# One transformer layer with routed experts on one core: row scatters at eight places instead of one, and a new order of the first keys and queries

## The reference

```
q,k,v = x @ qkv_w.T            16 heads of 16 channels
q,k   = rotary(q), rotary(k)   x*cos + rotate_half(x)*sin
attn  = softmax(q k^T / 4 + 8 * slope_h * min(0, key - query))
x1    = layernorm(x + (attn v) @ proj_w.T + proj_b)
shared= silu(x1 @ sW1 + sb1) @ sW2 + sb2
act   = sqrt(softplus(x1 @ routing_W.T + expert_bias));  top 2 of 8 experts
out   = layernorm(x1 + shared + sum over the 2 of act_e * expert_e(x1))
```

## Time and profile before

| | |
|---|---|
| median of the runs | 1753.69 us |
| the profiled execution's own time | 1758.38 us |
| its span | 1756.6 us |
| granted clock of PE, mean | 0.916 of full |
| PE busy | 1494.1 us, 85% |
| DVE busy | 1161.4 us, 66% |
| ACT busy | 1031.6 us, 59% |
| POOL busy | 723.8 us, 41% |
| first score product | 38.26 us |

### The profile page before, as it was taken

One profiled execution on the slowest core, in us unless ns is written; L12 is line 12 of the kernel. 1 busy time (PEld: TensorE's weight loads), 2 busy tenths in 40 slices (PEclk: granted clock), 3 DMA queues, 4 the chain that ended last, 5 costly groups with the idle time before them and its releaser, 6 DMA issues.

```text
span 1756.6 us, 33407 instructions
## 1 busy us (share of the span) xinstructions
PE 1494.1 (85%) x11096; PEld 812.6 (46%) x11096; DVE 1161.4 (66%) x2641; ACT 1031.6 (59%) x1766; POOL 723.8 (41%) x662
## 2 busy tenths in 40 slices
PE   3887989898898999999889998888999897977764
PEld 1433434444454454544445554444444454545643
DVE  5775767676877575666776776758767665533356
ACT  0265656565566576766656675656656675753633
POOL 0233354544435434343545535363354533232444
PEclk7699999899899999999999999999998998977887
DMA  5335243333343444444454545445454555436853
GB/s 181 100 118 160 81 123 101 105 115 111 96 135 122 138 137 148 134 143 140 134 167 155 163 138 165 149 144 164 141 152 148 177 163 178 122 117 190 272 187 118
DMA packets 189924, 251.74 MB, mean 143 GB/s; under 512 B 67837, under 2 KB 104794, under 8 KB 189754
## 3 DMA queue, kind: packets, MB, share of 16 engines
q1 hardware_dynamic: 177514, 216.96, 40.4%
q0 software_dynamic: 11520, 31.47, 5.6%
q10 hardware_dynamic: 720, 1.16, 0.2%
HBM read 157.78 MB, written 95.90 MB: 144 GB/s over the span
## 4 chain that ended last, share of the span: by engine, by line
PE 54%; DVE 14%; SPq 11%; DMA 8%; issue 7%; another core or an unknown queue 3%; ACT 2%; POOL 1%; ACTq 0%; DVEq 0%; POOLq 0%
PE pS L605 15%; PE pV L648 10%; DVE negm L893 6%; PE pG L670 5%; PE pG L781 3%; PE pG L679 3%; PE pS L611 3%; DMA rb<-d_rec 2%; DMA d_rec<-scr 2%; PE pG L773 2%; PE pG L692 2%; SPq L410 2%; PE pG L754 2%; SPq L454 2%
## 5 line engine op out<-in xcount | busy, mean ns | idle before, releaser
L893 DVE TENSOR_REDUCE negm<-pS 128x1 f32<-128x512 f32 x1024 | 660.2, 683 | 351.7 <-PE pS L611 296.8
L1294 ACT ACTIVATE ee<-pT,slp 128x512 f32<-128x512 f32 x1024 | 651.0, 684 | 271.3 <-PE pT L632 212.9
L605 PE MATMUL pS<-ka,qa 62*128 62x512 f32 x1024 | 491.8, 512 | 162.1 <-DVE negm L893 103.9
L626 PE MATMUL pT<-qa,ka 64*128 64x512 f32 x1024 | 489.9, 511 | 12.4 <-ACT ee L1294 11.4
L605 PEld LDWEIGHTS pS<-ka,qa 62*128 62x128 f32 x1024 | 199.9, 195 | 409.8 <-issue 361.9
L648 PE MATMUL pV<-ee,vv 128*32 128x512 f32 (+1 forms) x2048 | 295.9, 652 | 1.5 <-issue 1.2
L611 PE MATMUL pS<-mAB,tri 64*128 64x64 bf16 x2048 | 244.7, 201 | 0.0
L632 PE MATMUL pT<-mAB,tri 64*128 64x64 bf16 x2048 | 241.8, 199 | 0.0
L1450 POOL TENSOR_TENSOR raw<-raw,rope 128x512 f32<-128x512 f32 x60 | 76.8, 1280 | 366.5 <-DVE sh L923 366.5
L626 PEld LDWEIGHTS pT<-qa,ka 64*128 64x128 f32 x1024 | 198.0, 193 | 25.7 <-issue 13.2
L611 PEld LDWEIGHTS pS<-mAB,tri 64*128 64x128 bf16 x2048 | 120.5, 100 | 137.5 <-issue 99.2
(11 more groups left out here) (175 smaller groups left out, 2128.1 us busy)
## 6 DMA issues: line engine op xcount, KB each, us to landing
d_part<-parts SPq DMA_DIRECT2D x64, 512.0 KB
qa<-d_part SPq DMA_DIRECT2D x384, 64.0 KB
wb<-in_wb SPq DMA_DIRECT2D x88, 256.5 KB
xg<-d_x SPq DMA_DIRECT2D x88, 256.0 KB
d_y<-yb SPq DMA_DIRECT2D x88, 256.0 KB
ka<-d_part SPq DMA_DIRECT2D x128, 128.0 KB
xT<-in_xT SPq DMA_DIRECT2D x16, 512.0 KB
ka<-d_part SPq DMA_DIRECT2D x128, 64.0 KB
```

The source lines that it names most:

```text
L605: e.matmul(pS[:, k, :], qa[g % 4][r, i, t * 128:t * 128 + 128].bitcast(F32R), ka[g % 4][r, i, :].bitcast(F32R), start=True, stop=False)
L626: e.matmul(pT[:, k, :], ka[g % 4][r, i, kt * 128:kt * 128 + 128].bitcast(F32R), qa[g % 4][r, i, :].bitcast(F32R), start=True, stop=False)
L893: e.tensor_reduce(negm[:, g % 2, j, t + k:t + k + 1], pS[:, k, :], AX, ALU.max, negate=True).then_inc(s_max, 1)
L1294: e.activation(ee[:, w % 2, k, j, :], pT[:, k, :], ACT.Exp, scale=slp[:, 6, h:h + 1]).then_inc(s_exp, 1)
```

## The change

1. **Scatters.** `SCATTER` is now (78, ..., 85): one indirect DMA in each of eight slots. The waits before the first stay before the first.
2. **The start.** The key and query weights come in slices; the loads of `xT` and the first rows of `bpos` come earlier; masks are made on POOL behind the first two rotations. DVE does the rotations of i = 0, 1 and 2 of block 0, i = 1 directly behind i = 0 in tiles of its own (`raw_q`, `sh_q`, `parts_q`, which lie in `gg` and `bs`); i = 3 goes to POOL. `bpos` is made for four heads first (DVE), for the rest by ACT. Part of the row loads of groups 0 and 1 is issued by ACT.
3. **Idle products.** `warm(n)` makes n products of zeros (128 x 256) in front of the first real product, between products and around the wait before the first score.
4. **Later weights.** `LATE` is 11, the five preparations of `PREP` are at 18, 20 and 22, SP's part of them at 24. `load_xT(1)` is in slot 3.

```diff
-SCATTER = (81, 81)
+SCATTER = (78, 79, 80, 81, 82, 83, 84, 85)
-LATE, PREP, PADS = 3, 8, 40
+LATE, PREP, PADS = 11, (18, 20, 22, 24), 40
+WARM = (5, 6, 4, 4, 5)
...
+    def query_rows(e, g, some):
+        q_ = d_part[g // 4 % 2][0, 4 * (g % 4):4 * (g % 4) + 4]
+        for a in some:
+            for c in range(2):
+                r0 = 64 * c
+                e.dma_start(qa[g % 4][r0:r0 + 32, a, :], q_[2 * a + c, :, 0:1, :].broadcast_to([D, 2, T])
+                            ).then_inc(qk_in[g % 4], 16)
+            r0 = 64 * a + 32
+            e.dma_start(qa[g % 4][r0:r0 + 16, :, :], q_[a::2, :, 1, :].rearrange("a d t -> d a t")).then_inc(qk_in[g % 4], 16)
...
@@ stream of SP @@
+        def key_rows(g):
+            k_ = d_part[g // 4 % 2][1, 4 * (g % 4):4 * (g % 4) + 4]
+            for c in range(2):
+                r0 = 64 * c
+                e.dma_start(ka[g % 4][r0:r0 + 32, :, :], k_[c::2].rearrange("a d p t -> (d p) a t")).then_inc(qk_in[g % 4], 16)
+                e.dma_start(ka[g % 4][r0 + 32:r0 + 48, :, :], k_[c::2, :, 0, :].rearrange("a d t -> d a t")
+                            ).then_inc(qk_in[g % 4], 16)
         def assemble(g):
             if g > 3:
                 e.wait_ge(s_t, 16 * (g - 3))
-            if 0 < g < 4:
-                bias_rows(g)
-            e.wait_ge(p_w, 16 * (4 * (g // 4) + 2 * (g % 4 // 2) + 2))
...
+            if g == 1:
+                e.wait_ge(s_bias2, 4)
+                bias_out(slice(32, 128), slice(4, H))
+            if g == 2:
+                e.wait_ge(b_w, 64)
+            if g in (2, 3):
+                bias_rows(e, g)
+            if g:
+                e.wait_ge(p_k0, 16)
+            e.wait_ge(p_w, 16 * (4 * (g // 4) + 2 * (g % 4 // 2) + 1))
+            query_rows(e, g, range(2) if g > 1 else range(1))
+            if g:
+                key_rows(g)
...
+        e.dma_start(wqkv[:, :, 256:384], w_[:, :, 256:384]).then_inc(l_k0, 16)
         load_xT(0)
+        e.dma_start(wqkv[:, :, 0:128], w_[:, :, 0:128]).then_inc(l_q0, 16)
         e.dma_start(rope[:, 0, :], A["k_cos"]).then_inc(l_rope, 16)
         e.dma_start(rope[:, 1, :], A["k_sin"]).then_inc(l_rope, 16)
+        e.dma_start(wqkv[:, :, 384:768], w_[:, :, 384:768]).then_inc(l_qkv, 16)
+        e.dma_start(wqkv[:, :, 128:256], w_[:, :, 128:256]).then_inc(l_qkv, 16)
         e.wait_ge(s_bias, 1)
+        bias_out(slice(0, 32), slice(0, 4))
         e.wait_ge(b_w, 32)
+        bias_rows(e, 0)
...
                     parts_out(b, i)
+                    if 4 * b + i == 1:
+                        e.wait_ge(p_k0, 16)
+                        key_rows(0)
...
@@ stream of PE @@
+        def warm(n):
+            for _ in range(n):
+                e.matmul(pT[:, 0, 0:C], zb[:, 0:128], zb[:, 0:C], start=True, stop=True)
         def score_wait(s):
+            if s == 0:
+                warm(WARM[3])
+                e.wait_ge(p_w, 16)
+                warm(WARM[4])
             g = s // 8
             e.wait_ge(qk_in[g % 4], group_in(g))
             if s == 0:
+                e.wait_ge(l_tri, 32)
                 e.wait_ge(s_slope, 4)
...
@@ stream of DVE @@
+        def split_queries():
+
+            shuffle(0, 1)
+            e.wait_ge(s_sh, 2)
+            link(e.tensor_tensor(raw_q, raw_q, rope[:, 0, :], ALU.mult))
...
             for i in range(4):
                 if (b := due(s, QK[i][-1] + SHUFFLE)) >= 0:
-                    shuffle(b, i)
-                    if b == 0:
+                    if 4 * b + i != 1:
+                        shuffle(b, i)
+                    if b == 0 and i in (0, 2):
                         rotate(i)
+                    if b == 0 and i == 0:
+                        split_queries()
+                        scale_queries(1)
...
@@ stream of ACT @@
                     qk(b, i)
+                    if 4 * b + i == 1:
+                        e.wait_ge(s_slp, 1)
+                        e.wait_ge(l_pos2, 16)
+                        for r in (slice(32, 64), slice(64, 128)):
+                            for r0 in (0, 21):
+                                e.activation(bpos[r, r0:r0 + 7, :], bpos[r, r0:r0 + 7, :], ACT.Copy, scale=slc[r, 0:1]
+                                             ).then_inc(s_bias2, 1)
+                    if 4 * b + i == 2:
+                        e.wait_ge(p_w, 16)
+                        query_rows(e, 0, range(1, 2))
+                    if 4 * b + i == 3:
+                        query_rows(e, 1, range(1, 2))
+                        e.wait_ge(b_w, 64)
+                        bias_rows(e, 1)
...
@@ stream of POOL @@
+        e.wait_ge(s_part, 2)
+        e.wait_ge(s_slp, 1)
+        e.wait_ge(l_tri, 32)
+        for half_ in range(2):
...
+            for k in range(2):
+                m_ = msk[r, k, :].rearrange("p (a j) -> p a j", a=1).broadcast_to([64, 8, 64])
+                e.tensor_tensor(mAB[r, k, :, :], m_, c_, ALU.mult).then_inc(s_slope, 1)
+                e.wait_ge(s_slope, 2 * half_ + k + 1)
...
-            for n in range(2):
-                if 0 <= (b := due(s, SCATTER[n])) < SPARSE:
-                    scatter(b, n)
+            for k in range(8):
+                if 0 <= (b := due(s, SCATTER[k])) < SPARSE:
+                    scatter(b, k)
...
-                    if (b := due(s, QK[i][-1] + ROPE[k])) > 0:
+                    if 4 * (b := due(s, QK[i][-1] + ROPE[k])) + i > 2:
                         rotate(4 * b + i, k)
```

More of the change, by code:

```diff
@@ L299, in _build @@
     bias2 = [yb[0][0:E + 1, 0, :], yb[0][0:E + 1, 1, :], yb[1][0:E + 1, 0, :]]
+    raw_q, sh_q = (gg[i][:, :, :].rearrange("p k c -> p (k c)") for i in range(2))
+    parts_q = bs[0][:, :, :].rearrange("p (k t) c -> p k (t c)", k=2)
     hot = ee[:, 0, 1, 0, 0:H]
@@ L371, in _, with bias_out @@
     def _(e):
[L372 to L377, removed]
+        def bias_out(r, h):
+            for k in range(2):
+                e.dma_start(d_bias[k][:, h].rearrange("r h (c e) -> (h c) r e", c=8), bpos[r, 14 * k:14 + 16 * k, :]
+                            ).then_inc(b_w, 16)
         def load_xT(b):
@@ L1163, in add_expert @@
                     link(e.bn_stats(st[:, 2, t, :], x1[b % 2][:, t, :]))
+        e.memset(zb[:, 0:C], 0.0).then_inc(s_zb0, 1)
+        e.wait_ge(s_zb0, 1)
+        for x in (*rb2, sb2):
+            last = e.tensor_copy(x[:, :].bitcast(F32R), zb[:, 0:C])
+        last.then_inc(s_zero, 1)
         for i in range(2):
@@ L1168, in _ @@
         e.memset(pV[:, :], 0.0)
-        link(e.memset(zb[:, 0:C], 0.0))
-        linked()
-        for x in (*rb2, sb2):
-            last = e.tensor_copy(x[:, :].bitcast(F32R), zb[:, 0:C])
-        last.then_inc(s_zero, 1)
         e.memset(minus[:, :], -0.5)
@@ L1197, in _, with scale_queries @@
         link(e.scalar_tensor_tensor(P(6), P(3), 0.25, P(6), ALU.mult, ALU.mult))
-        e.wait_ge(l_qkv, 16)
-        for c in range(2):
-            q_ = wqkv[:, c, 0:256].rearrange("p (h d) -> p h d", h=H)
-            last = e.tensor_tensor(q_, q_, P(5).rearrange("p (h a) -> p h a", a=1).broadcast_to([128, H, D]), ALU.mult)
-        last.then_inc(s_qscale, 1)
+        linked()
+        def scale_queries(k):
+            e.wait_ge((l_q0, l_qkv)[k], (16, 32)[k])
+            q_ = wqkv[:, :, 128 * k:128 * k + 128].rearrange("p c (h d) -> p c h d", d=D)
+            c_ = P(5)[:, 8 * k:8 * k + 8].rearrange("p (c h a) -> p c h a", c=1, a=1).broadcast_to([128, 2, 8, D])
+            e.tensor_tensor(q_, q_, c_, ALU.mult).then_inc(s_qscale, 1)
+        scale_queries(0)
         e.wait_ge(l_pos, 32)
@@ L1306, in qk @@
             e.wait_ge(g_full[bk("qk", i, b)], full("qk", i, b))
-            if 4 * b + i:
-                e.wait_ge(s_part, 4 * b + i)
-            e.copy(raw[:, :], pG[bk("qk", i, b)][:, :]).then_inc(g_free[bk("qk", i, b)], 1)
+            n = 4 * b + i
+            if n > 1:
+                e.wait_ge(s_part, n - 1 if n == 2 else n)
+            e.copy(raw_q if n == 1 else raw[:, :], pG[bk("qk", i, b)][:, :]).then_inc(g_free[bk("qk", i, b)], 1)
         def v(b, j):
@@ L1445, in rotate @@
         def rotate(n, k):
-            r = steps * (n - 4)
+            r = steps * (n - 3)
             if k == 0:
@@ L1473, in rstd, with scatter @@
             e.tensor_tensor(off[:, k, :], nm[:, k, :], rs[:, k, :], ALU.mult).then_inc(s_pow[k], 1)
-        def scatter(b, n):
+        def scatter(b, k):
             g = GROUP_OF[b]
-            if n == 0:
+            n, t = divmod(k, 4)
+            if k == 0:
                 e.wait_ge(s_x1, b + 1)
@@ L1483, in scatter @@
                         e.wait_ge(xg_in[i], 16 * ((FIRST_BLOCK[g - 1] + 2 - i) // 3))
-            for t in range(4):
-                e.indirect_dma_start(d_x[g % 2], bass.IndirectOffsetOnAxis(pos[:, b % 2, n, t:t + 1], 0),
-                                     x1[b % 2][:, t, :], None).then_inc(rows_w, 16)
+            e.indirect_dma_start(d_x[g % 2], bass.IndirectOffsetOnAxis(pos[:, b % 2, n, t:t + 1], 0),
```

(1 more changed line is left out.)

112 lines of the change are left out of this document (61 added, 51 removed).

## The result

The changed kernel takes 1705.28 us (median, 1700.56 to 1707.97), the kernel before 1754.63 beside it: ratio 0.970 [0.966, 0.975]. That is 49 us by the medians and 52 by the ratio. 1707 had been forecast. The profiled execution after took 1707.97 us (span 1705.9), the one before 1758.4. So the number was met. The experiments show that this was in part luck: of the two parts of the sum one was sized too large and the other too small.

What follows compares the result with a forecast made beforehand. PE's order of work, busy 85%, was taken to set the end, with idleness at the start and scatters. 1758.4 - 16.6 - 30 + 1 = 1712.8; less 4.7, 1708.1; with 1 us for half-clock time, 1707 us; range 1672 to 1743.

Steps and rivals of the forecast that it cites:

- The start: Work from the first score through the preparations: 16.6 us saved together, from 10 to 25.
- The scatters: POOL's bursts of eight, spread over slots: 60% of 50 us of PE stalls and half clock goes, 30 us; bounds 0 and 50.
- First score: Start of block 0: the last row landing before the scores moves from 38.2 to 25.4, 12.8 us earlier; upper bound 14.
- Second rotation: Rotation in slot 1, moved to POOL: PE's 3.59 us wait for it shrinks to the shuffle, 2.8 us saved.
- rival C: SP's queue, slots 16 to 48: late loads give back the start's gain, 6 instead of 16.6, time 1717; chance 0.13.
- SP's wait for the two writes, 0 to 2: SP's wait for prepared rows moves from slot 8 to slot 24, before row maxima: cost 0 to 2 us.
- Preparations: Five operations, 1.3 us together, move from where DVE bounds to where PE does: 1 us saved, between 0 and 1.3.
- Idle products: Before the first score, to raise PE's clock: taken as 0, since PE stayed at 1.2 GHz in the scores; upper bound 8.
- Rival A: Cost belongs to each scatter, so stalls move with them; only the start's gain remains: 1737, 1734 to 1745; chance 0.19.
- Pushed work: Later last scatter makes DVE wait at `base` in thirteen blocks: 1 us cost, upper bound 21.
- Rival B: Last scatter becomes DVE's wait at `base`, slots 87 and 89: slower, 1773; chance 0.06.
- Rival D: All stalls go: 50 us from the scatters, 22 from the start with the clock up, 1682; chance 0.14.

Runs made afterwards that it cites:

- scatters-only kernel: The kernel before with only the scatters placed one per slot, 78 to 85, its start untouched: 1713.28 us, ratio 0.973.
- the two runs of four: The kernel before with four scatters at slot 81 and four at slot 83: 1728.3 us, ratio 0.981.

## Why the prediction was right, and where not

The total of 1707 against 1705 hides two mis-sized terms. **The start** was 16.6 and measured 7.5 (2.5 to 12.5), below the lower bound of 10 by its middle. **The scatters** were 30 and measured 48 (40 to 56), close to the upper bound of 50. The forecast sum of the parts was 46.6, the whole measured 49 to 52, and the parts measured alone add to 55. That the total fits to 2 us is luck: the errors of 9 and 18 us had opposite signs, and the whole measured a little less than its parts, within the noise.

*First score, 12.8: measured 10.1.* `xT` came as worked out (product at 6.55 for 7). DVE's shuffle stood at 11.0 where I had 10, and that was in my own terms: 7, 3.4 for the product and 0.6 for the copy make 11. Then DVE stood 1.38 us for the sine half of `rope`, which I had not looked for; queries were ready at 20.2 for 18. With the 0.5 us of the idle products that is the 2.7 that is missing. POOL's four mask products took 5.46 us for my 5.2, 20.34 to 25.8, and were not what ended the wait: the rows landed at 27.7, as the kernel without idle products shows. Beside them DVE's rotation of the next keys took 1.53 and 1.42 us for operations of 0.69 each.

*Second rotation, 2.8: 0.* The 3.59 us went from their place, and 3.79 stand at group 4 instead. This is rival C's mechanism, to which I gave 0.13 and 10.6 us; a third of that came. The step that failed is "SP's wait for the two writes, 0 to 2": I asked who stands right behind the wait (row maxima), not who stands last in the queue (group 4's rows). The kernel with the wait at slot 44 shows the cause: slot 31 is 2.2 us long in it for 5.8. The one with the wait at slot 32 and the pads moved wins 7.4 us by slot 64.

*Preparations, 1:* too small to be read. *Idle products, 0:* right, 0.5 lost and 0.7 won. The granted clock was 0.99 in the two slots behind them and 0.50 in the next 14 us, of which PE was busy 12.68. The Trainium skill (TensorE: Matmul & The Clock Gate, What's actually happening) has activity release the throttle; in this case it did for the run of idle products, and the scores behind them did not keep it. The prediction took the row's side, 0 and not 4.2, and that held.

*Scatters, 60% of 50: nearly all.* The mechanism, POOL's order and the mean of the stretches were right; the share was not. I had argued that a run of five in 8.3 us is near the old rate. The kernel with spaced DMAs shows that one in 2.4 us costs next to nothing, and eight scatters in 18 us are at that rate. Runs of two or three within it pass: of the 8.6 us of idleness left in the ten stretches, 5.8 are in the first three. Rival A is refuted by the scatters-only kernel and, for the mechanism, by the spaced one. What the prediction made of the Trainium skill (SBUF — State Buffer, SBUF: two separate sides), that a queue of scatters stalls nobody, is refuted too. The page itself speaks of the two sides of SBUF only; no row shows where the stall arises, so nothing here speaks for or against it.

*Pushed work, 1:* the landing ended two waits of DVE, 0.6 us together. Rival B did not come. *Rival D* is where the scatters went, without the start.

What stays open: why indirect DMAs of POOL at one in 1.27 us hold PE up, and whether a slow rate alone helps or other work of POOL between them is needed. Seen are PE's slots becoming longer, DVE and ACT getting PE's results late by "remote", and no dependence on bytes or direction. The plain DMAs, sent faster, leave 1.5 of 6.8 us to the bytes and the sending of a POOL DMA as such. What is left is what the indirect ones have beside them: the list of 128 indices, and rows at scattered addresses, where the plain ones wrote rows that follow each other. No run here parts these two, and no view shows which part of the handling meets PE. The ends of matmuls are modelled, so a late end and a late signal can't be told apart. And of the 15 us between the scatters-only kernel and the two runs of four, one stretch explains about 5 (that block is 101.6 us long for 96.6).

## What to carry to other kernels

Count the indirect DMAs in a row, gathers and scatters together; put other work of the same engine between them, down to one in some 2.4 us here, and don't expect smaller rows to help. When a waiting instruction is moved in a queue, follow the queue to the transfer that PE needs, however far behind it stands. And when a forecast is met, run the parts alone: here they were off by 9 and 18 us.

## What the runs showed of the hardware that was not expected

- A close run of eight indirect DMAs costs 6.8 us, half of it by PE's idleness and half by its clock. Four cost 1.2 to 1.6, eight spaced ones 0.1 us of PE's busy time in 20 us, with the clock lower in two of the eight stretches. Rows of 8 bytes read, 256 and 1024 bytes written give the same.
- Two plain DMAs that write 2 MB each from ACT's queue kept DVE 6.8 us waiting for loads of SP's queue, with the DMA engines busy all the time.
- DVE's operations of 0.69 us took up to 1.53 beside four bf16 products of POOL (64x512). The Trainium skill (SBUF — State Buffer, SBUF: two separate sides) gives DVE and GpSimd one pair of ports that either holds alone, DVE for operations with two inputs in SBUF while GpSimd reads it. The trace agrees: 1.53 and 1.42 against 0.69.
